# Squares of the adjacency from GpSimd to ScalarE, three of eight high halves of the gates to VectorE

## The reference

```
L0:  h = relu(A @ (f1 * (A @ (x @ W1))));  u = A @ (f2 * (A @ (h @ W2)))
L1:  u = concat([x, A @ x]) @ Wcat
L2:  m = x @ W_msg + b_msg;  q = m @ W_q;  k = m @ W_k
     g = sigmoid(q @ k.T / sqrt(128) + gate_bias) * A * A        # adj serves as adjacency and as recency prior
     u = layernorm(relu(concat([x, g @ m]) @ W_upd + b_upd)) * gamma + beta
L3:  s = swish((A @ x) @ W + b);  u = swish((A @ s) @ W + b)
each layer:  x = layernorm(x + u)
```

## Time and profile before

| | |
|---|---|
| time, median of 3 runs | 1895.87 us (1895.03 to 1899.65) |
| span of the profiled execution | 1896.7 us |
| busy: TensorE, VectorE, ScalarE, GpSimd | 89%, 79%, 53%, 25% |
| gated pass, first gate to last low half | 935.0 to about 1491 us |
| read from memory | 420.32 MB, 223 GB/s over the span |

### The profile page before, as it was taken

How to read it: one execution, slowest core, us unless ns; L and a number is a source line. 1 busy time by engine, 2 the same in 40 slices (tenths; PEclk the granted TensorE clock), 3 DMA queues, 4 the chain that set the end, 5 groups by cost and what they waited for, 6 DMA issues and landing times.

```text
span 1896.7 us, 18699 instructions
## 1 busy us (share of the span) xinstructions
PE 1683.2 (89%) x7618; PEld 776.0 (41%) x7618; DVE 1494.3 (79%) x1231; ACT 1007.3 (53%) x709; POOL 471.2 (25%) x187
## 2 busy tenths in 40 slices
PE   7999999999999899898978786786786879999986
PEld 4444444444444444444433342242232434444432
DVE  6874565537556974788999999999999997654997
ACT  5764455446445543655646654554554756553753
POOL 1000000000000210112475656756756140000022
PEclk9999999999999999999989988888888999999999
DMA  9986776647766756666723433333333679764983
GB/s 374 391 315 232 258 312 248 240 176 285 268 243 230 280 206 239 246 246 240 266 89 133 149 118 111 118 126 111 112 132 111 240 252 353 286 232 171 351 304 139
DMA packets 59206, 423.64 MB, mean 223 GB/s; under 512 B 6800, under 2 KB 6960, under 8 KB 8304
## 3 DMA queue, kind: packets, MB, share of 16 engines
q1 hardware_dynamic: 57888, 417.88, 59.8%
q0 software_dynamic: 1088, 4.49, 0.7%
q10 hardware_dynamic: 144, 0.07, 0.0%
HBM read 420.32 MB, written 2.10 MB: 223 GB/s over the span
## 4 chain that ended last, share of the span: by engine, by line
PE 51%; DVE 34%; issue 9%; ACT 2%; POOL 1%; DMA 1%; SPq 0%; POOLq 0%; DVEq 0%; ACTq 0%
PE acc L502 32%; PE spare L502 15%; DVE gates L867 10%; DVE a_lo L851 9%; DVE a_lo L843 7%; ACT a_hi L677 2%; DVE bn L773 2%; PE rows L415 1%; PE rows L408 1%; DMA a_ring<-adj_dram 1%; DVE stats L784 1%; POOL x_rows L918 1%; DVE stats L787 1%; PE rows L421 1%; DVE moments L776 1%
## 5 line engine op out<-in xcount | busy, mean ns | idle before, releaser
L843 DVE SCALAR_TENSOR_TENSOR a_lo<-a_ring,a_hi 128x2048 f16<-128x2048 f32 x332 | 777.3, 2365 | 308.2 <-ACT a_hi L677 307.8
L677 ACT ACTIVATE a_hi<-a_ring 128x2048 f16<-128x2048 f32 x332 | 630.0, 1907 | 419.1 <-PE spare L502 275.1
L502 PE MATMUL acc<-a_hi,y_hi 128*128 128x512 f16 x1584 | 488.1, 390 | 157.9 <-DVE a_lo L851 121.4
L502 PE MATMUL acc<-a_hi,y_lo 128*128 128x512 f16 x1584 | 489.8, 391 | 0.0
L502 PE MATMUL acc<-a_lo,y_hi 128*128 128x512 f16 x1584 | 489.5, 391 | 0.0
L957 POOL TENSOR_TENSOR a_ring<-a_ring 128x1024 f32<-128x1024 f32 x112 | 312.1, 2813 | 97.2 <-DMA a_ring<-adj_dram 97.2
L909 POOL TENSOR_TENSOR val<-val,moments 128x1024 f32<-128x1024 f32 x19 | 51.2, 2694 | 1027.6 <-DVE moments L776 1027.6
L502 PEld LDWEIGHTS acc<-a_hi,y_hi 128*128 128x128 f16 x1584 | 150.2, 99 | 367.6 <-DVE a_lo L851 153.5
L685 ACT ACTIVATE a_hi<-gates 128x1024 f16<-128x1024 f32 x128 | 135.2, 1056 | 246.1 <-DVE gates L867 246.1
L851 DVE TENSOR_TENSOR a_lo<-gates,a_hi 128x1024 f16<-128x1024 f32 x128 | 263.5, 2058 | 0.0
L867 DVE SCALAR_TENSOR_TENSOR gates<-gates,a_ring 128x1024 f32<-128x1024 f32 x128 | 258.6, 2021 | 0.0
(11 more groups left out here) (111 smaller groups left out, 979.3 us busy)
## 6 DMA issues: line engine op xcount, KB each, us to landing
a_ring<-adj_dram SPq DMA_DIRECT2D x396, 1024.0 KB, 5.1
x_T<-xt_dram SPq DMA_DIRECT2D x4, 512.0 KB, 8.1
x_rows<-x_dram POOLq DMA_DIRECT2D x1, 2048.0 KB, 10.6
out_dram<-x_rows POOLq DMA_DIRECT2D x3, 512.0 KB, 4.6
out_dram<-x_rows SPq DMA_DIRECT2D x2, 256.0 KB, 2.0
w<-W_dram POOLq DMA_DIRECT2D x2, 64.0 KB, 5.4
wcat<-Wcat_dram POOLq DMA_DIRECT2D x1, 128.0 KB, 7.0
wupd<-W_upd_dram POOLq DMA_DIRECT2D x1, 128.0 KB, 7.6
```

The lines of the kernel that those rows point to most:

```text
L502: mm = pe.matmul(sums[:, h * BANK:(h + 1) * BANK], blk(y[:, y_pass % 2, :], j), slot(a, st)[:, s, h * BANK:(h + 1) * BANK], start=(begins ...
L677: act.activation(slot(a_hi, st), loaded(st), ACT.Copy, scale=2.0 ** A_EXP).then_inc(s_ahi, 1)
L843: dve.scalar_tensor_tensor(out=slot(a_lo, st).rearrange("p s c -> p (s c)"), in0=loaded(st).rearrange("p s c -> p (s c)"), scalar=2.0 ** A ...
```

## The change

- All squares go to ScalarE, one instruction for a whole step of two blocks (128x2048): the first step's before the first sigmoid, each further step's after the second sigmoid of the step before it, behind the high half issued there. GpSimd keeps its layer norm stages and has no squares.
- The high half of gates 1, 4 and 6 of every eight (HIGH_BY_VECTOR) is made by VectorE with a `tensor_copy`, right behind the low half of the gate before; that is 48 of 128.
- The semaphores follow: one for the squares, counted by steps, and one for the high halves of each engine.
- The layer norm's instructions, the rings and the loads are unchanged.

```diff
--- before.py
+++ after.py
@@ -32,7 +32,7 @@
 GATED = 6
 AHEAD = 4
 LONE_LOGITS = 5
-ACT_SQUARES = 8
+HIGH_BY_VECTOR = (1, 4, 6)


 A_EXP = 10
@@ -239,8 +239,9 @@
         s_id0, s_id = sem("ident_zero"), sem("ident_ready")
         s_ahi, s_alo, s_unit = sem("a_hi_ready"), sem("a_lo_ready"), sem("unit_multiplied")
         s_lg, s_pr = sem("logits_ready"), sem("probs_ready")
-        s_sq, s_sqa = sem("squares_by_gpsimd"), sem("squares_by_scalar")
-        s_g, s_ghi, s_glo = sem("gates_ready"), sem("g_hi_ready"), sem("g_lo_ready")
+        s_sq = sem("step_squared")
+        s_g, s_glo = sem("gates_ready"), sem("g_lo_ready")
+        s_ghi_act, s_ghi_dve = sem("g_hi_by_scalar"), sem("g_hi_by_vector")
         s_rows, s_xT = sem("rows_written"), sem("x_T_saved")
         s_zt, s_val, s_nl, s_sw = sem("z_T_ready"), sem("val_ready"), sem("nonlinearity_done"), sem("swish_done")
         s_res, s_aff = sem("residual_added"), sem("affine_done")
@@ -332,6 +333,19 @@

         def gated_index(st, s):
             return (st.n - GATED_FROM) * SJ + s
+
+        def high_by_vector(u):
+
+            return u % 8 in HIGH_BY_VECTOR
+
+        def highs_by_vector(u):
+
+            return sum(high_by_vector(v) for v in range(u))
+
+        def slot_free(u):
+
+            before = STREAM[GATED_FROM + u // SJ - RING]
+            return LAST_USE[before.n] + 1 - (SJ - 1 - u % SJ if before.p == GATED else 0)

         def in_idle_sums(u):

@@ -677,12 +691,16 @@
                 act.activation(slot(a_hi, st), loaded(st), ACT.Copy, scale=2.0 ** A_EXP).then_inc(s_ahi, 1)

             def gate_high(u):
+                if high_by_vector(u):
+                    return
                 st = STREAM[GATED_FROM + u // SJ]
                 act.wait_ge(s_g, u + 1)
-
-                before = STREAM[st.n - RING]
-                act.wait_ge(s_unit, LAST_USE[before.n] + 1 - (SJ - 1 - u % SJ if before.p == GATED else 0))
-                act.activation(slot(a_hi, st)[:, u % SJ, :], gates[:, u % G_RING, :], ACT.Copy).then_inc(s_ghi, 1)
+                act.wait_ge(s_unit, slot_free(u))
+                act.activation(slot(a_hi, st)[:, u % SJ, :], gates[:, u % G_RING, :], ACT.Copy).then_inc(s_ghi_act, 1)
+
+            def square(st):
+                act.wait_ge(s_a[st.n % LOADS], 16 * (st.n // LOADS + 1))
+                act.activation(loaded(st), loaded(st), ACT.Square).then_inc(s_sq, 1)

             for st in STREAM:
                 if st.p != GATED:
@@ -692,9 +710,8 @@
                 for s in range(SJ):
                     u = gated_index(st, s)
                     at = epilogue(stages, at, FIRST_USE[st.n] + s - AHEAD + 1)
-                    if u % ACT_SQUARES == ACT_SQUARES - 1:
-                        act.wait_ge(s_a[st.n % LOADS], 16 * (st.n // LOADS + 1))
-                        act.activation(loaded(st)[:, s, :], loaded(st)[:, s, :], ACT.Square).then_inc(s_sqa, 1)
+                    if u == 0:
+                        square(st)
                     act.wait_ge(s_lg, u + 1)
                     if u >= G_RING:

@@ -706,6 +723,8 @@
                                    scale=2.0 ** -(Q_EXP + K_EXP) * F ** -0.5).then_inc(s_pr, 1)
                     if u >= 1:
                         gate_high(u - 1)
+                    if s == SJ - 1 and u < NB * NC - 1:
+                        square(STREAM[st.n + 1])
                     if u == NB * NC - 1:
                         gate_high(u)
             epilogue(stages, at, THE_END)
@@ -845,9 +864,19 @@
                                          in1=slot(a_hi, st).rearrange("p s c -> p (s c)"), op0=ALU.mult,
                                          op1=ALU.subtract).then_inc(s_alo, 1)

+            def gate_high(u):
+                if high_by_vector(u):
+                    st = STREAM[GATED_FROM + u // SJ]
+                    dve.wait_ge(s_g, u + 1)
+                    dve.wait_ge(s_unit, slot_free(u))
+                    dve.tensor_copy(slot(a_hi, st)[:, u % SJ, :], gates[:, u % G_RING, :]).then_inc(s_ghi_dve, 1)
+
             def gate_low(u):
                 st = STREAM[GATED_FROM + u // SJ]
-                dve.wait_ge(s_ghi, u + 1)
+                if high_by_vector(u):
+                    dve.wait_ge(s_ghi_dve, highs_by_vector(u) + 1)
+                else:
+                    dve.wait_ge(s_ghi_act, u - highs_by_vector(u) + 1)
                 dve.tensor_tensor(slot(a_lo, st)[:, u % SJ, :], gates[:, u % G_RING, :], slot(a_hi, st)[:, u % SJ, :],
                                   ALU.subtract).then_inc(s_glo, 1)

@@ -860,15 +889,13 @@
                     u = gated_index(st, s)
                     at = epilogue(stages, at, FIRST_USE[st.n] + s - AHEAD + 1)
                     dve.wait_ge(s_pr, u + 1)
-                    if u % ACT_SQUARES == ACT_SQUARES - 1:
-                        dve.wait_ge(s_sqa, u // ACT_SQUARES + 1)
-                    else:
-                        dve.wait_ge(s_sq, u + 1 - u // ACT_SQUARES)
+                    dve.wait_ge(s_sq, u // SJ + 1)
                     dve.scalar_tensor_tensor(out=gates[:, u % G_RING, :], in0=gates[:, u % G_RING, :],
                                              scalar=2.0 ** G_EXP, in1=loaded(st)[:, s, :], op0=ALU.mult,
                                              op1=ALU.mult).then_inc(s_g, 1)
                     if u >= 1:
                         gate_low(u - 1)
+                    gate_high(u)
                     if u == NB * NC - 1:
                         gate_low(u)
             epilogue(stages, at, THE_END)
@@ -948,13 +975,7 @@
             pool.dma_start(x_rows[:, :, :], x).then_inc(s_x, 16)
             for st in STREAM[GATED_FROM:GATED_FROM + STEPS * NC]:
                 for s in range(SJ):
-                    u = gated_index(st, s)
                     at = epilogue(stages, at, freed(st) + s)
-                    if u % ACT_SQUARES == ACT_SQUARES - 1:
-                        continue
-                    pool.wait_ge(s_a[st.n % LOADS], 16 * (st.n // LOADS + 1))
-                    adj_block = loaded(st)[:, s, :]
-                    pool.tensor_tensor(adj_block, adj_block, adj_block, ALU.mult).then_inc(s_sq, 1)
             epilogue(stages, at, THE_END)

             for h in range(HALVES):

```

## The result

The changed kernel takes 1777.88 us (median of 4 runs, 1777.6 to 1779.71), the kernel before, run beside it, 1896.8. The ratio is 0.9373, 95% interval 0.936 to 0.9386. The forecast was 1780. The profiled execution spans 1775.9 us, 120.8 less than before.

What follows compares the result with a forecast made beforehand. VectorE was taken to bound the gated pass, slowed by GpSimd's squares. Savings of 42.7 (first window), 57.8 (middle), 13.8 (last) and 1 (start), 115 us off 1896.7, gave 1781, forecast as 1780 us, range 1752 to 1802.

Steps and rivals of the forecast that it cites:

- The price of a square: Gated pass: each of 112 GpSimd squares takes 1.70 us out of VectorE, 190 us in all.
- Squares on ScalarE at no cost: Gated pass: 64 squares of 1.80 us bring ScalarE to 82.7 us a chunk, below VectorE's share, so the average costs nothing.
- The rival of the lumps: Gated pass: VectorE's next gate waits behind ScalarE's 1.8 us squares; half exposed 58 us, total 1838 us; chance 0.12.
- Copies at 1.135: Gated pass: 48 high-half copies on VectorE at 1.135 us each, 13.6 us a chunk, 54 us in all.
- the 12 us that the prediction drew from it: With the skill's 0.6 us a copy, 54 us of copies would be 29 and the total some 12 us lower.
- Middle chunks: Two 32-gate stretches of the gated pass: 114.4 us each against 143.3, 57.8 us saved for the two.
- the account by lines: VectorE's work in a middle chunk, summed item by item: 72.6 + 12.3 + 11.3 + 13.6 = 109.8 us.
- First window: First 43 gates of the gated pass: VectorE 131.3 us plus 3.7 of waits, 135.0 against 177.7, 42.7 saved.
- Last window: Last 21 gates of the gated pass: 76.9 us of VectorE plus 1, 77.9 against 91.7, 13.8 saved.
- Sum: Whole kernel: savings 42.7 + 57.8 + 13.8 + 1 = 115 us off the profiled 1896.7, giving 1781.
- The start: Start of the gated pass: pass 5's last splits lose their squares, the first sigmoid follows a 1.8 us square; 1 us saved.
- The rival of a low clock: Gated pass: PE stays at 1.2 GHz, 5.1 us a gate in place of 2.59, total 2007 us; chance 0.03.

Runs made afterwards that it cites:

- squares that nobody waits for: The changed kernel plus 98 square-sized GpSimd multiplications on other tiles, whose results nobody in the gated pass waits for: 1923.9 us.
- copies-alone kernel: The kernel before with the high halves of gates 1, 4, 6 of eight on VectorE and the squares left on GpSimd: 1924.4 us.
- smaller pieces: The changed kernel with ScalarE's squares issued block by block, 128 of 0.95 us in place of 64 of 1.8: 1770.4 us.
- slow copies: The changed kernel with its 48 VectorE copies written as a two-source maximum of the gate with itself: 1793.9 us.

## Why the prediction was right, step by step

**The price of a square, 1.70 us of VectorE.** Right, and now shown without any wait for the square's data: squares that nobody waits for cost it too. The middle chunk of the copies-alone kernel, 150.5, is the 143.3 of before plus 12 x 0.60.

**Squares on ScalarE at no cost.** Nearly right. Taking them out gains 16 us of 115, of which I had put none beside the waits. About half of it goes with smaller pieces. The rival of the lumps had the right mechanism and a price (58 us half exposed, against some 8) seven times too high. That the sigmoids' lead of several gates covers most of them is likely, but no run changed that lead.

**Copies at 1.135.** The term that was mis-sized: 0.60 measured. At 48 copies that is 26 us of VectorE's time, and 16 of the total (1793.9 against 1777.9). The estimate of 0.6 from the Trainium skill ("VectorE: DVE Perf Modes", perf-mode tier table) was right, although the table's row is for a copy within fp32 and this one goes to fp16; the trace of the changed kernel agrees with it, and the 12 us that the prediction drew from it compare with these 16.

**Middle chunks: 114.4 forecast, 110.2 measured.** VectorE's work came out 6.4 lower by the copies; its idle time was 7.4, not 4.6. With slow copies the chunk is 114.0, VectorE 109.05 busy for the 109.8 of the sum, so the account by lines was right and only its input was off.

**First window: 135.0 forecast, 147.9 measured.** The other mis-sized term, and the larger one. I had summed VectorE and added 3.7 of waits; it idled 25. With the copies at 0.60 that sum is 122.7, and VectorE was busy 122.7; the fault is in what was taken to lie beside it. PE was busy 136.8 of 147.9. The prediction put PE at 43 x 2.59 = 111 and four times 3.58 for pass 5's end, 126 together, and said that it stays below, when the earlier trace rows already had PE 141.3 busy in that window. That VectorE isn't the limit there the slow copies show: 8.4 us more of its work made the window 2.7 longer. ScalarE's squares cost it 4.7 (143.3 in the kernel without squares). No run changed PE's part.

And it begins badly. These are ScalarE and PE of the changed kernel at the pass's start:

```profile
926.54 1.89 ACT L703 ACTIVATE a_ring<-a_ring 128x2048 f32<-128x2048 f32 x1
928.45 1.28 ACT L722 ACT_TABLE_LOAD   x1
929.74 1.11 ACT L722 ACTIVATE gates<-spare,gbias 128x1024 f32<-128x1024 f32 x1
933.69 1.11 ACT L722 ACTIVATE gates<-spare,gbias 128x1024 f32<-128x1024 f32 x1 [2.84 <-PE spare L539]
...
944.46 1.02 ACT L614 ACTIVATE z_T<-acc 128x1024 f32<-128x1024 f32 x1 [5.36 <-PE acc L516]
945.38 1.11 ACT L722 ACTIVATE gates<-spare,gbias 128x1024 f32<-128x1024 f32 x1
```

```profile
930.91 1.04 PE L539 MATMUL spare<-qT_hi,kT_hi 128*128 128x512 f16 x2 [2.40 <-ACT gates L722]
...
946.54 0.60 PE L539 MATMUL spare<-qT_hi,kT_hi 128*128 128x512 f16 x2 [2.12 <-ACT gates L722]
```

PE waits 2.40 us for the first sigmoid, 0.60 before: the new square stands in front of it, and PE's next four pairs of matmuls take 1.04 to 1.06 each in place of 0.59, half the clock. The fourth sigmoid stands behind the evacuation of pass 5's last sums, which waits 5.36 us for PE; then PE waits 2.12 for that sigmoid. The kernel before has this second wait too, but there it lay beside VectorE's turns with GpSimd, which kept VectorE busy throughout:

```profile
946.19 0.60 PE L525 MATMUL spare<-qT_hi,kT_hi 128*128 128x512 f16 x2 [2.12 <-ACT gates L705]
946.29 2.91 DVE L851 TENSOR_TENSOR a_lo<-gates,a_hi 128x1024 f16<-128x1024 f32 x1
```

With that cover gone it comes out: VectorE idles 5.03 before the fourth gate. That this order of ScalarE's queue costs what it seems to was not tried.

**Last window: 77.9 forecast, 71.6 measured.** 4.3 us of it are the eight copies; the rest is VectorE's account, which was 2.2 too high there (70.4 busy for 72.6 with cheap copies), as it was for the kernel before (93.3 by the same terms and 15 squares, 91.0 busy).

**Sum.** The start and first window came out 10 us too low (start at 931, not 934; window 12.9 longer), the two middle windows 8.4 and the last 6.3 too high. They nearly cancel: 1781 for 1775.9 of the profile. That the total is so close is luck. At the prediction's own price of a copy the kernel takes 1793.9, 14 over the 1780, mostly because the first window is 15.7 longer than the sum had it; the copies, cheaper than taken, gave 16 back. Inside the stated range are both.

**PE's clock.** The rival of a low clock was rightly held to be small: the granted clock in the middle windows rose from 0.87 and 0.86 to 0.94 and 0.95, and to 0.97 where VectorE has the layer norm as well. The spells at half clock that I read in the changed kernel's middle chunks follow waits for `a_lo` in the layer norm's stretch, as before:

```profile
1091.80 1.04 PE L516 MATMUL acc<-a_hi,y_hi 128*128 128x512 f16 x2 [3.58 <-DVE a_lo L880]
```

The Trainium skill's rule ("TensorE: Matmul & The Clock Gate", HAM oscillation) has waits of TensorE bring such spells; the trace agrees, with TensorE's idle time before `a_lo` down from 121.4 us to 42.9 and the clock up.

## What to carry to other kernels

Before work goes to an idle GpSimd, compare what its instruction takes out of VectorE (1.70 us here for 128x1024 float32) with what VectorE would need for it itself (1.14): where VectorE is the limit, the helper can cost more than it carries, even at 25% busy and with nobody waiting for it. When one engine's account adds up to half a per cent, it can be rewritten line by line, but only for the stretches where it is the limit afterwards too; each window has to be asked which engine comes next, and what stood in the shadow of the old limit. Whether half of a change is worth having can depend on the other half: the copies lost 28 us alone and gained 7 together.

## What the runs showed of the hardware that I had not expected

A VectorE copy from float32 to float16 takes about half the time of a two-source instruction of the same shape: 0.60 us between neighbours against 1.14, both 128x1024 in SBUF. It takes turns with GpSimd like the others (2.38 us beside an instruction of it). And six GpSimd instructions moved to VectorE made VectorE's busy time smaller, 98.6 us a chunk against 102.8.
